# A decoder's last attention projects its output by seven of eight block products, and table values are chosen on GpSimd

## The reference

```python
# layer 0, "attention": a gated MLP in which the smaller half of |silu| is zeroed per token
s = silu(x @ w_gate.T)                       # 1376 values per token
_, idx = top_k(-abs(s), 688); s[rows, idx] = 0.0
x = x + (s * (x @ w_up.T)) @ w_down.T

# layer 0, third part: router over 64 experts of rank 8
scores = (x @ Wq.T) @ keys.T
gate = softmax over the 16 largest scores, zero elsewhere
x = x + ((x @ A.T) * gate, per expert) @ B.T * scaling

# layer 3, cross-attention: 32 query heads of 128, 8 key heads, RMS norm on q and k
kv = concatenate([context, latents])
q, k, v = rms(latents @ Wq), rms(kv @ Wk), kv @ Wv
out = softmax(q k^T / sqrt(128)) @ v         # 4 query heads share a key head
x = x + out @ Wo                             # 4096 -> 512

# layer 3, third part: a linear layer whose weights are 4-bit codes into a table of 16 values per row
w_l = take_along_axis(lut4, code)            # 512 x 512, code 0..15
x = x + (x @ w_l.T or, for large tokens, x @ w_h.T) + bias
```

## Time and profile before

| | us |
|---|---|
| median of 3 runs (4019.86 to 4023.96) | 4022.04 |
| profiled execution | 4018.64 |
| its span, first to last instruction | 4016.8 |
| last attention, in the span | 3210 to 3965 |
| first attention | to 557 |
| router | 993 to 1140 |

### The profile page before, as it was taken

One profiled execution on the slowest core, in us unless ns is written; L12 is line 12 of the kernel. 1 busy time (PEld: TensorE's weight loads), 2 busy tenths in 40 slices (PEclk: granted clock), 3 DMA queues, 4 the chain that ended last, 5 costly groups with the idle time before them and its releaser, 6 DMA issues. The chain is left out here.

```text
span 4016.8 us, 53404 instructions
## 1 busy us (share of the span) xinstructions
PE 3841.4 (96%) x20108; PEld 2233.6 (56%) x20108; DVE 2496.8 (62%) x4200; ACT 1411.9 (35%) x2537; POOL 770.5 (19%) x734
## 2 busy tenths in 40 slices
PE   8899999998999899998999999899999999999998
PEld 4344445554466577776677754455555555555564
DVE  0889965553247455556858658877767565665563
ACT  2888845553223211111213434211112133333232
POOL 1111111111001444445320111122112110000000
PEclk9999999999999999999999999999999999999999
DMA  5111121101110433311010022100010011111110
GB/s 191 53 43 43 56 79 32 35 30 61 40 37 14 176 126 106 129 56 76 1 71 1 1 109 63 62 22 22 22 43 22 10 61 37 37 37 37 43 37 24
DMA packets 133975, 215.54 MB, mean 54 GB/s; under 512 B 42576, under 2 KB 95056, under 8 KB 123104
## 3 DMA queue, kind: packets, MB, share of 16 engines
q1 hardware_dynamic: 133728, 212.19, 15.2%
HBM read 168.12 MB, written 44.04 MB: 53 GB/s over the span
## 5 line engine op out<-in xcount | busy, mean ns | idle before, releaser
L1345 PE MATMUL l3a_po<-l3a_wo,l3a_cT 128*128 128x512 f32 x512 | 229.5, 596 | 1.2 <-ACT l3a_cT L1546 1.2
L1345 PEld LDWEIGHTS l3a_po<-l3a_wo,l3a_cT 128*128 128x128 f32 x512 | 95.6, 190 | 119.9 <-issue 115.5
L851 DVE TENSOR_TENSOR x<-x,l1x_po 128x512 f32<-128x512 f32 (+1 forms) x154 | 88.4, 582 | 88.5 <-PE l1x_po L642 87.7
L1126 POOL TENSOR_TENSOR l3x_ws<-l3x_wq 128x256 f32<-128x256 f32 x16 | 13.3, 834 | 578.7 <-DMA l3x_wo<-in_L_xattn_Wo 376.7
L1229 PE MATMUL l3x_pj<-kvT,l3x_ws 128*128 128x512 f32 x256 | 120.4, 602 | 2.3 <-DVE l3x_qT L1676 2.2
L2840 POOL TENSOR_TENSOR l0x_q<-l0x_q,l0x_qi 128x512 f32<-128x512 f32 x64 | 65.4, 1042 | 298.3 <-DVE l0x_qi L3129 298.3
L1229 PE MATMUL l3a_pj<-kvT,l3a_ws 128*128 128x512 f32 x256 | 120.8, 605 | 0.8 <-ACT l3a_saves L1488 0.8
L1345 PE MATMUL l3x_po<-l3x_wo,l3x_cT 128*128 128x512 f32 x256 | 115.3, 593 | 0.7 <-ACT l3x_cT L1546 0.7
L1345 PE MATMUL l3x_pc<-l3x_wo,l3x_cT 128*128 128x512 f32 x256 | 115.2, 593 | 0.0
L2387 DVE TENSOR_SCALAR_CACHE_REDUCE l0a_keep<-l0a_keep,l0a_scalars 128x1376 uint16<-128x1376 uint16 x64 | 105.4, 1646 | 3.6 <-DVE l0a_scalars L2393 1.5
L1643 DVE TENSOR_TENSOR l3a_part<-l3a_raw,l3a_sinq 64x512 f32<-64x512 f32 x128 | 102.8, 803 | 4.0
(11 more groups left out here) (667 smaller groups left out, 9207.5 us busy)
## 6 DMA issues: line engine op xcount, KB each, us to landing
l1x_kb<-l1x_keys SPq DMA_DIRECT2D x32, 512.0 KB, 4.7
l1x_vb<-l1x_values SPq DMA_DIRECT2D x32, 512.0 KB, 3.5
l1x_keys<-l0a_kv SPq DMA_DIRECT2D x40, 256.0 KB, 2.0
fill_wk<-in_L_xattn_Wk SPq DMA_DIRECT2D x8, 1024.0 KB, 5.5
kvT<-in_L_xattn_Wv SPq DMA_DIRECT2D x8, 1024.0 KB, 5.6
l1x_values<-l0a_kv SPq DMA_DIRECT2D x32, 256.0 KB, 2.3
l1x_wq<-in_L_xattn_Wq SPq DMA_DIRECT2D x8, 1024.0 KB, 5.8
l1x_sbias<-in_L_xattn_bias SPq DMA_DIRECT2D x8, 1024.0 KB, 7.3
```

The costliest lines, as they stand in the source:

```text
L851: nc.vector.tensor_tensor(dst, dst, src, ALU.add).then_inc(added, 1)
L1345: mm = pe.matmul(outs[t % 2][:, :], cT[:, h, t * P:(t + 1) * P], wo[:, u, h, :], start=h == 0, stop=h == GH - 1)
```

## The change

Four edits:
1. In the last attention the output projection goes by pairs of tiles: seven products of 128x256 in place of eight of that size. `out_low` and `out_high` issue them, in phases a, p, b, q, c, and VectorE's `add_block` adds a bank after each phase, five additions for two. POOL prepares the differences: `mix_cols(n)` of the weights, four operations of 128x512 once per group, and `mix_rows(n, tt)` of the attended rows, four of 128x256 per pair. One of the two value pieces of a group moves ahead of the last two parts of the projection.
2. The picks of the table's values go from VectorE to POOL: values 1 to 8 of a row block in an odd group, 9 to 15 in the next even one, and all 15 of the last block in group 7. Bits and code stay on VectorE, in other places of the group.
3. In the first attention the 24 spins ahead of tile 1's gate become 6 ahead of tile 2's, and the 8 behind it move to tile 2. ScalarE does two probes fewer beside tile 0 at one place.
4. In the router the last quarter of a filler unit moves behind the transposes of zg, into the wait for zT; ScalarE copies that unit after zT. At the start the transposes of the first tile stand between two filler units.

```diff
+                def picks(oc, lo, hi):
+                    row = m.wl[:, oc, :]
+                    pool.wait_ge(coded, LOWB * (oc + 1) + 1)
+                    for v in range(lo, hi):
+                        if oc or v > 1:
+                            pool.wait_ge(picked, picked_at(oc, v) + 1)
+                        nc.gpsimd.tensor_scalar(pick[:, v % 2, :], code[:, :], float(v), lut[:, oc:oc + 1, v], ALU.is_equal,
+                                                ALU.mult).then_inc(picked, 1)
+                        pool.wait_ge(picked, picked_at(oc, v) + 2)
+                        nc.gpsimd.tensor_tensor(row, row, pick[:, v % 2, :], ALU.add).then_inc(picked, 1)
+
+                def mix_cols(n):
...
+                    pool.wait_ge(w_loaded[u], 8 * loads * (n + 2 - u))
+                    if n:
+                        pool.wait_ge(o_ready, out_at(n - 1, 3, "c") + 2)
+                    nc.gpsimd.tensor_tensor(wos[:, 0], high, low, ALU.subtract).then_inc(cols_mixed, 1)
...
+                def mix_rows(n, tt):
...
+                    pool.wait_ge(a_copied, 2 * STEPS * n + 2 * tt + 3)
...
+                    nc.gpsimd.tensor_tensor(cs[:, v, 0], one, one2, ALU.subtract).then_inc(rows_mixed, 1)
...
                     mix(n, 1)
                     if rope:
                         join(n, 1)
+                    if rms:
+                        if n:
+                            for tt in range(T // 2):
+                                mix_rows(n - 1, tt)
+                        mix_cols(n)
                     if n + 1 < GROUPS:
                         mix(n + 1, 0)
+                    if rms and n == GROUPS - 1:
+                        picks(n // 2, 1, 1 << LOWB)
+                    elif rms and n % 2:
+                        picks(n // 2, 1, 9)
+                    elif rms and n:
+                        picks(n // 2 - 1, 9, 1 << LOWB)
+                if rms:
+                    for tt in range(T // 2):
+                        mix_rows(GROUPS - 1, tt)
...
+                def out_low(n, u, tt):
+                    one, two2 = attended_rows(0, 2 * tt), attended_rows(1, 2 * tt + 1)
...
+                    product(first_bank(n, tt), one, out_block(u, 0, 0), True).then_inc(o_ready, 1)
+                    if tt:
+                        pe.wait_ge(added, out_at(n, tt - 1, "q") + 2)
+                    pe.wait_ge(cols_mixed, cols_at(n, 4) + 2)
+                    product(po2[:, 0:256], two2, wos[:, 2], True)
+                    pe.wait_ge(rows_mixed, rows_at(n, tt, 1) + 2)
+                    product(po2[:, 256:512], attended_rows(0, 2 * tt + 1), out_block(u, 0, 1), True).then_inc(o_ready, 1)
+
+                def out_high(n, u, tt):
+                    v, two = tt % 2, attended_rows(1, 2 * tt)
+                    pe.wait_ge(rows_mixed, rows_at(n, tt, 2) + 2)
+                    pe.wait_ge(added, out_at(n, tt, "a") + 2)
+                    product(first_bank(n, tt), cs[:, v, 1], wos[:, 1], False).then_inc(o_ready, 1)
+                    pe.wait_ge(rows_mixed, rows_at(n, tt, 4) + 2)
+                    pe.wait_ge(added, out_at(n, tt, "p") + 2)
+                    product(po2[:, 256:512], cs[:, v, 2], out_block(u, 1, 1), False)
+                    product(po2[:, 0:256], two, out_block(u, 1, 0), True).then_inc(o_ready, 1)
+                    pe.wait_ge(added, out_at(n, tt, "b") + 2)
+                    product(first_bank(n, tt), cs[:, v, 0], wos[:, 0], False).then_inc(o_ready, 1)
...
                 def gate_up(n):
                     if n == 0:
                         pe.wait_ge(loaded, 32)
-                    elif n == 1:
-                        spin(pe, m, f.po, 24)
+                    elif n == 2:
+                        spin(pe, m, f.po, 6)
...
-                        for g in filled(n):
+                        for g in filled(n)[:-1]:
                             fill.unit(pe, g)
+                        fill.unit(pe, filled(n)[-1], 0, KC - 1)
...
                     mm.then_inc(z_turned, 1)
+                    if not last(n):
+                        fill.unit(pe, filled(n)[-1], KC - 1, KC)
                     pe.wait_ge(zT_ready, n + 2)
```

More of the change, by code:

```diff
@@ new lines, in out_part @@
+                def out_part(n, u, i):
+                    if rope:
+                        out(n, u, i)
+                    elif i % 2:
+                        out_high(n, u, i // 2)
+                    else:
+                        out_low(n, u, i // 2)
+                def rest_of_out(n, u):
+                    if rms:
+                        attend(n, 1)
+                        for tt in range(STEPS):
+                            out_low(n, u, tt)
+                            if tt + 2 < STEPS:
+                                attend(n, tt + 2)
+                            out_high(n, u, tt)
+                        return
@@ L1361, in group @@
                 def group(n, u, behind, more):
-                    held = 5 if not more else T
                     if behind:
@@ L1411, in group @@
                             pe.wait_ge(pair_read, pair(n, 1) + 2)
-                        out(n - 1, 1 - u, 5)
+                        out_part(n - 1, 1 - u, 5 if rope else 4)
                     turns(n, 1)
+                    if rms and not more:
+                        out_part(n - 1, 1 - u, 5)
                     if more:
@@ new lines, in add_part, with spread_bits @@
+                def add_part(n, i):
+                    if rope:
+                        add(n, i)
+                    else:
+                        for phase in "bqc" if i % 2 else "ap":
+                            add_block(n, i // 2, phase)
+                def spread_bits(oc, half):
+                    if oc == 0 and half == 0:
+                        dve.wait_ge(code_loaded, 32)
+                    elif half == 0:
+                        dve.wait_ge(coded, LOWB * oc + 1)
+                    for s in range(16 * half, 16 * half + 16):
+                        ins = nc.vector.tensor_scalar(bits[:, :, :, s], packed[:, oc:oc + 1].rearrange("p a b w -> p (a b) w"), s, 1,
+                                                      ALU.logical_shift_right, ALU.bitwise_and)
+                    ins.then_inc(bits_spread, 1)
@@ L1848, in group @@
                     if not more:
-                        add(n - 1, 5)
+                        add_part(n - 1, 5 if rope else 4)
                     weighed(n, 2)
-                    unpack(n, 3)
+                    if rms and not more:
+                        add_part(n - 1, 5)
                     if more:
@@ L2323, in even @@
                                 probes(n - 1, low - 2, low)
-                        more = done + beside.get(k, 0)
+                        more = done + (beside if n else beside_first).get(k, 0)
                         probes(n, done, more)
@@ L2571, in body @@
                     mm.then_inc(f.out_ready, 1)
-                for g in filled(-1):
-                    fill.unit(pe, g)
+                fill.unit(pe, filled(-1)[0])
                 f.turn(pe, 0)
+                fill.unit(pe, filled(-1)[1])
                 pe.wait_ge(loaded, 64)
```

222 lines of the change are left out of this document (147 added, 75 removed).

## The result

The changed kernel takes 4056.3 us (median of 4 runs, 4051.59 to 4059.54) against 4020.95 for the kernel before (4 runs). The ratio is 1.0093, 95% interval 1.0081 to 1.0105: slower by 0.9%, where 0.35% was forecast. 4056.3 lies above the range of 4020 to 4052. The profiled execution took 4056.84 us with a span of 4054.8, 38.0 longer than before.

The account below looks back on a forecast made before the run. TensorE, busy 96% of the span, was taken to bound the kernel. Groups −1.1, group 7 0, closing +26.5, first attention −6.3, router −5.0 gave +14.1 us: 4032.7 profiled, 4036 for the median, range 4020 to 4052.

Parts of the forecast that it names:

- the price of a pick: Closing, on POOL: one-input operation 0.69 us plus two-input addition, 2.12 us a pick with gaps; fifteen take 31.8 us.
- X: End of the last product of group 6's output in the last attention, forecast at 3924.4, 1.6 us later than before.
- Rival 2: POOL's one-input pick costs as a two-input operation: +8.7 us in the closing, total 4045 or more; chance 0.17.
- The closing's range: Last attention's closing: TensorE idles some 28 us for POOL's chain; +26.5 us, range 24 to 34.
- The 11.3 us: Gains forecast in layer 0: first attention −6.3 us and router −5.0 us, both counted in the final sum.
- The body: Last attention, groups 1 to 6: saving 19.7 us, less transfer, addition and port costs, sum −1.1 us.
- The 4.2 us for the additions of phase b: Groups 1 to 6: a pair's last product waits for VectorE's addition, 0.7 us a group, six groups.
- the transfer: Groups 1 to 6: TensorE waits about 0.35 us a group for the next weights, 2.1 us in all.
- The port: Groups 1 to 6: POOL's picks lengthen VectorE's joins and last weighting, about 2.05 us a group, 12.3 in all.
- Layer 0 and the router: First attention −6.3 us from fewer spins and an earlier first search; router −5.0 us from six tiles 0.84 earlier.

## Why the prediction was wrong

**The step that failed is the price of a pick.** Mechanism, place and order were right: thirty chained operations between two kinds of differences, behind X. Moving them took the wait away, and making them 9.3 us cheaper made it 9.3 us shorter. I priced the one-input operation at 0.69 us from the nearest row with seven elements and the slope of a MEMSET, bounded by 0.53 and 1.27. It took 2.00, outside both bounds: 15 × 1.31 = 19.7 of the 20.2 us by which this term was too small. A MEMSET's slope says nothing of an operation that compares, and the two-input addition is no upper bound for a one-input operation. Rival 2 had the direction and its "4045 or more" holds the result, but it stopped at 1.27, which is 8.7 of the 19.7. The closing's range, 24 to 34, didn't even reach its own bound of 35.2. The Trainium skill's GPSIMD Engine Reference, section 3.1, has 769 ns for 512 elements at best. The measurements decide here: the copy and the multiplication with an addition are faster than that (0.61 and 0.62), a lone comparison takes 1.49 and the pick's operation 2.00.

**Nothing was budgeted for an untouched stage.** The 11.3 us that I credited to layer 0 and the router were there, and more (−14.2 before the cross-attention gave back 1.7). I let them run through 2600 us to the end. Layer 2's third part gave back 13.3: earlier arrival, a longer wait for the same transfer, and the lower clock for 33 us. I had read the low clock in the earlier trace rows behind an idle time of 5.96 us and applied it to the closing alone.

**The body was better than forecast**, −7.2 against +0.5 at X, by misses that partly cancel. The 4.2 us for the additions of phase b didn't come (no such wait in groups 1 to 6), the transfer cost 1.2 in two groups in place of 2.1 in six, and group 1 gained 3.9 us that I hadn't seen: VectorE's dequantising had held TensorE there for 1.64 and 2.24 us, which is gone with it and is back in the kernel with the picks on VectorE. The port was right in kind and place, but its term was three times too large: 4.0 us for a forecast of 12.3. Each hit cost nearly twice what I took (0.95 for 0.5), but one operation a group was hit on TensorE's path where I charged four, and none in period 5. That they overlapped at all is luck of a kind: at my price the picks would have ended at about 3572, just where the joins begin (3575.8 less 3.3). POOL's late mix, 7.4 us over three groups with eight picks, was not in the sum; with picks at 2.12 us, eight would end, by estimate, some 12 us sooner (8 × 2.12 from 3549.8) and the mix would not have been late. The Trainium skill's SBUF — State Buffer, section on the two separate sides of SBUF, holds for the join: with two SBUF inputs, it waits until POOL's addition is done but for 0.14 us. The 32 operations on the packed bits, which more than double beside POOL, have one SBUF input each; whether the same lock holds them up, no run shows.

**Layer 0 and the router** were right, −7.9 and −6.3 for −6.3 and −5.0: the gate of tile 1 starts at 75.48, the first search at 100.47 for a forecast of about 100.7, and the router's output at 1009.59, with no wait. TensorE there, then VectorE, answering to the earlier trace rows:

```profile
1008.03 0.63 PE L2749 MATMUL l0f_pt<-ident,l0f_zg 128*128 128x128 f32 x4
1008.58 1.08 PE L2875 MATMUL l0f_fill<-kvT 128*64 128x512 f32 x4
1009.59 3.70 PE L2756 MATMUL l0f_po<-l0f_wb,l0f_zT 128*128 128x512 f32 x8
```

```profile
100.47 0.15 DVE L2563 COPY l0a_scalars<-bitsf 128x1 f32<-128x1 f32 x1 [74.92 <-ACT l0a_a L2398]
```

Open: the smaller shifts in layer 1's third part (+2.6 in the changed kernel, up to +5.5 in others) weren't followed, and nothing here says why a wait of 1.27 us is harmless and one of 1.88 is not in most executions. It isn't the length of an idle time alone: in every trace TensorE also idles 1.88 us at the border of the two stages, some 4 us earlier, and the clock stays up behind it.

## What to carry to other kernels

When work moves to an engine with room, look for the one place where its queue stands between two things that the critical engine needs; fifteen picks there held TensorE for 47 us, and with eight of them a few lines earlier and seven on VectorE the closing lost 5.6. An operation that no row shows at its size and kind has no upper bound from another kind: widen the range, or choose the order in which its price doesn't matter. And a gain upstream must be followed through each wait for a transfer behind it, since a microsecond more of idle can cost thirteen by the clock.

## What the runs showed of the hardware

- POOL's one-input operation on 128x512 float32: copy 0.61 us, multiply and add 0.62, multiply alone 1.50, compare alone 1.49, multiply by a value per row 1.57, compare and multiply 1.93 to 2.00; an instruction with two arithmetic operations took less than half the time of one with a single multiplication.
- A two-input product on POOL took 1.04 us for 128x512, sums and differences 1.26 to 1.27.
- VectorE's addition of two SBUF operands took 0.69 us alone and 1.64 beside POOL's addition: longer by what was left of POOL's operation, less 0.14 us (0.67, 1.09, 1.10 and 1.26 left for 0.53, 0.95, 0.96 and 1.12).
- On VectorE, 32 operations on packed bits took 3.40 us alone and 7.27 beside POOL's operations.
- TensorE's granted clock fell to the lower level for some 33 us behind idle times of 1.88 to 2.32 us (six traces), and stayed up behind 0.94 and 1.27, and with the wait filled by spins, in the same place.
